# Attention denominators: DMA accumulation replaced by adds on GpSimd and more ones-matmuls

## The reference, cut to what matters

```python
att = jnp.einsum('bhgqd,bhkd->bhgqk', q, k) / scale
att = jax.nn.softmax(att, axis=-1)
y = jnp.einsum('bhgqk,bhkd->bhgqd', att, v)
```

## Time and profile before

| what | value |
|---|---|
| median of three runs | 3620.76 us |
| the profiled execution's own time | 3621.32 us |
| its span, first to last instruction | 3619.7 us |
| PE busy | 3493.0 us, 96% |
| VectorE busy | 2232.6 us, 62% |
| ScalarE busy | 1593.6 us, 44% |
| GpSimd busy | 1602.2 us, 44% |
| mean granted TensorE clock | 0.978 |
| adding DMAs (L706) | 128, 1024 KB each, median 7.2 us to landing |

### The profile page before, as it was taken

The page is one execution under the profiler, slowest core; times in us unless marked ns, Lnnn a source line. Parts: engine busy times, 40 slices in busy tenths (PEclk is TensorE's granted clock), DMA queues, the critical chain, the costliest instruction groups (busy, mean ns, idle before and its releaser), DMA issues. The chain is left out here.

```text
span 3619.7 us, 46130 instructions
## 1 busy us (share of the span) xinstructions
PE 3493.0 (96%) x17196; PEld 2320.7 (64%) x17196; DVE 2232.6 (62%) x3725; ACT 1593.6 (44%) x2990; POOL 1602.2 (44%) x700
## 2 busy tenths in 40 slices
PE   6999899999999999999999889799999999999999
PEld 4778455555555555555555268688888888887787
DVE  5541877777777777777777178544444444442627
ACT  3210266666666666666666533222222222213544
POOL 1111288898889989898899800000000000000010
PEclk8999699999999999999999989899999999999999
DMA  6662455656555555555554444711111111113222
GB/s 226 204 186 82 114 118 103 124 107 120 108 109 119 112 113 112 120 109 118 108 108 93 96 151 172 204 30 29 29 30 29 29 30 29 29 41 117 90 66 85
DMA packets 196074, 361.96 MB, mean 100 GB/s; under 512 B 41728, under 2 KB 122880, under 8 KB 175680
## 3 DMA queue, kind: packets, MB, share of 16 engines
q0 software_dynamic: 37104, 202.92, 24.7%
q1 hardware_dynamic: 156496, 154.69, 15.6%
q10 hardware_dynamic: 2304, 2.10, 0.2%
HBM read 162.13 MB, written 62.78 MB: 62 GB/s over the span
## 5 line engine op out<-in xcount | busy, mean ns | idle before, releaser
L772 DVE TENSOR_REDUCE att_chunk_max<-att_scores 128x1 f32<-128x512 f32 x2048 | 1268.9, 683 | 349.7 <-PE att_scores L843 347.5
L753 ACT ACTIVATE att_exp<-att_scores_T 128x512 f32<-128x512 f32 x2048 | 1042.7, 603 | 507.4 <-PE att_scores_T L857 503.4
L697 POOL TENSOR_TENSOR att_exp_pair<-att_exp 128x2048 f32<-128x2048 f32 x256 | 1198.6, 4727 | 133.1 <-ACT att_exp L753 132.8
L843 PE MATMUL att_scores<-att_k_stack,att_q_stack 96*128 96x512 f32 x2048 | 875.8, 450 | 16.7 <-DMA att_q_stack<-q_scratch 12.9
L857 PE MATMUL att_scores_T<-att_q_stack,att_k_stack 98*128 98x512 f32 x2048 | 745.3, 402 | 3.3 <-ACT att_exp L753 3.2
L843 PEld LDWEIGHTS att_scores<-att_k_stack,att_q_stack 96*128 96x128 f32 x2048 | 392.1, 192 | 427.2 <-DVE att_chunk_max L772 267.9
L868 PE MATMUL att_y_acc<-att_exp,att_v_head 128*32 128x512 f32 x4096 | 494.4, 600 | 0.0
L857 PEld LDWEIGHTS att_scores_T<-att_q_stack,att_k_stack 98*128 98x128 f32 x2048 | 386.4, 189 | 148.4 <-ACT att_exp L753 63.5
L1229 POOL DMA_DIRECT2D inter_scratch<-gu_inter x84 | 45.2, 538 | 884.6 <-DVE gu_inter L1172 884.6
L1283 ACT ACTIVATE gu_magnitude<-gu_value 128x512 f32<-128x512 f32 x88 | 55.7, 633 | 516.7 <-DVE gu_value L1314 516.7
L1313 DVE TENSOR_TENSOR gu_rounded<-gu_up_acc,gu_rounded 128x512 f32<-128x512 f32 x88 | 60.9, 692 | 323.7 <-PE gu_up_acc L1348 323.7
(11 more groups left out here) (191 smaller groups left out, 4925.1 us busy)
## 6 DMA issues: line engine op xcount, KB each, us to landing
att_exp_pair<-att_exp_pair POOLq DMA_DIRECT2D x128, 1024.0 KB, 7.2
att_q_stack<-q_scratch SPq DMA_DIRECT2D x96, 256.0 KB, 5.7
shared_raw<-in_wd_t POOLq DMA_DIRECT2D x34, 256.0 KB, 3.5
qkv_x_tile<-in_x SPq DMA_DIRECT2D x16, 512.0 KB, 4.8
q_scratch<-qkv_qk_out_hi POOLq DMA_DIRECT2D x32, 256.0 KB, 3.1
q_scratch<-qkv_qk_out_lo POOLq DMA_DIRECT2D x32, 256.0 KB, 4.3
qkv_wqkv_raw<-in_wmod POOLq DMA_DIRECT2D x8, 1024.0 KB, 7.4
qkv_wmod<-in_wmod POOLq DMA_DIRECT2D x8, 1024.0 KB, 8.2
```

The lines of the kernel that those rows point to most:

```text
L697: nc.gpsimd.tensor_tensor(ps[PAIR_SLOT[j]][:], pr[2 * j % NP][:], pr[(2 * j + 1) % NP][:], ALU.add).then_inc(pair_done, 1)
L753: nc.scalar.activation(pr[k % NP][:, h * NB:(h + 1) * NB], stp[bank(u, c, GH * k + h)][:], ACT.Exp, scale=INV_SQRT_DH).then_inc(exp_done, 1)
L772: nc.vector.reduce_max(cmax[c % 2][:, q:q + 1], turn_buffer(u, c, q)[:], AX.X).then_inc(sm_done, steps_done(u, q))
L843: nc.tensor.matmul(turn_buffer(u, c, q)[:], qs[c % 4][0:SR, h, qt * P:(qt + 1) * P], ks[c // QB % 2][0:SR, kc * NB:(kc + 1) * NB], start=T ...
```

## The change

The four adding DMAs and their semaphores go. POOL now makes two sums of four tiles, P0+P1 into buffer 0 behind P1, and P2+P3 into buffer 2 behind P3. The other four pair sums go to PE as they are, so PE has ND = 6 groups per unit. Three of them are issued in the unit's own loop, behind the bursts of k = 10, 12 and 14 (`DEN_AHEAD`), three in the next unit behind k = 0, 2 and 4 (`DEN_LATE`). The trip moves up: the copy on ACT to k = 4, the reciprocal on DVE to k = 8, `y_out` on POOL to behind P3 and ahead of the second sum. SP stores y ahead of the next unit's maxima.

```diff
--- before.py
+++ after.py
@@ -465,19 +465,16 @@
     NST = 3
     TQ = 6
     NP, NS = 8, 5
-    PAIRS = KT // 2
+    PAIRS, QUADS = KT // 2, 2
+    ND = QUADS + PAIRS - 2 * QUADS
     PAIR_SLOT = (0, 1, 2, 3, 4, 1, 3, 2)
-    DMA_SUM = ((0, 1), (2, 3), (0, 2), (3, 2))
-    SUM_PAIRS = (1, 3, 3, 7)
-    DMA_AFTER = {1: 0, 3: 1, 4: 2, 7: 3}
-    QUAD_AFTER = 5
-    DEN_SLOT = (0, 4, 3)
-    ND = len(DEN_SLOT)
-    DEN_AT = (0, 2, 6)
+    DEN_SLOT = (0, 2, 4, 1, 3, 2)
+    DEN_AHEAD = (10, 12, 14)
+    DEN_LATE = (0, 2, 4)
     RP = 8
-    DEN_COPY = 6
-    RECIP_AT = 9
-    Y_AFTER = 5
+    DEN_COPY = 4
+    RECIP_AT = 8
+    Y_AFTER = 3
     DW = GH * NB // P
     TSTEP = 14
     PER = NTURN // KT
@@ -516,8 +513,7 @@
         sm_ready, sm_done = sem("scores_ready"), sem("scores_consumed")
         mT_hi, m_stored = sem("max_T_hi"), sem("max_rows_stored")
         pv_done, pair_done, den_done = sem("pv_done"), sem("pair_done"), sem("den_done")
-        quad_done = sem("quad_sum_done")
-        dma_sum = [sem(f"dma_sum_done{i}") for i in range(len(DMA_SUM))]
+        quad_done = sem("quad_done")
         y_copied, y_done, y_stored = sem("y_copied"), sem("y_done"), sem("y_stored")
         const_done = sem("consts_done")
         den_copied, den_stored, den_loaded = sem("den_copied"), sem("den_stored"), sem("den_loaded")
@@ -661,10 +657,9 @@
                     load_v((c // QB + 1) % 2, g + 1)
                 if not is_first(u):
                     den_trip(u - 1, (c - 1) % BODY)
+                    store_y(u - 1, (c - 1) % BODY, g if c % QB else g - 1)
                 if not beyond(u, 1):
                     store_max(u + 1, c + 1)
-                if not is_first(u):
-                    store_y(u - 1, (c - 1) % BODY, g if c % QB else g - 1)
 
             units(sp, unit)
             sp.wait_ge(last_y, 1)
@@ -676,38 +671,14 @@
             def pair(u, j):
                 pool.wait_ge(exp_done, NST + 2 * GH * (j + 1) + u * NX)
 
-                if j == 0:
-                    pool.wait_ge(den_done, 1 + u * ND)
-                elif j == 1:
-                    if u:
-                        pool.wait_ge(quad_done, u)
-                elif j == 2:
-                    if u:
-                        pool.wait_ge(dma_sum[3], u * 16)
-                elif j == 3:
-                    pool.wait_ge(den_done, 3 + u * ND)
-                elif j == 4:
-                    pool.wait_ge(den_done, 2 + u * ND)
-                elif j == 5:
-                    pool.wait_ge(dma_sum[0], 16 + u * 16)
-                elif j == 6:
-                    pool.wait_ge(dma_sum[1], 16 + u * 16)
-                elif j == 7:
-                    pool.wait_ge(dma_sum[2], 16 + u * 16)
+                if j in (0, 1, 2):
+                    pool.wait_ge(den_done, (1, 4, 6)[j] + u * ND)
+                elif j == PAIRS - 1:
+                    pool.wait_ge(den_done, ND + 2 + u * ND)
+                elif j in (5, 6):
+                    pool.wait_ge(quad_done, j - 4 + u * QUADS)
                 nc.gpsimd.tensor_tensor(ps[PAIR_SLOT[j]][:], pr[2 * j % NP][:], pr[(2 * j + 1) % NP][:],
                                         ALU.add).then_inc(pair_done, 1)
-
-            def sum_by_dma(u, i):
-                into, other = DMA_SUM[i]
-                pool.wait_ge(pair_done, NP // 2 + SUM_PAIRS[i] + 1 + u * PAIRS)
-                if i == 2:
-                    pool.wait_ge(dma_sum[0], 16 + u * 16)
-                    pool.wait_ge(dma_sum[1], 16 + u * 16)
-                pool.dma_start(ps[into][:], ps[other][:], accum_op=ALU.add).then_inc(dma_sum[i], 16)
-
-            def quad_sum(u):
-                pool.wait_ge(pair_done, NP // 2 + 6 + u * PAIRS)
-                nc.gpsimd.tensor_tensor(ps[4][:], ps[4][:], ps[1][:], ALU.add).then_inc(quad_done, 1)
 
             def y_out(u, c):
 
@@ -719,12 +690,12 @@
             def unit(u, c, g):
                 for j in range(PAIRS):
                     pair(u, j)
-                    if j in DMA_AFTER:
-                        sum_by_dma(u, DMA_AFTER[j])
-                    if j == QUAD_AFTER:
-                        quad_sum(u)
                     if j == Y_AFTER and not is_first(u):
                         y_out(u - 1, c - 1)
+                    if j % 2 == 1 and j < 2 * QUADS:
+                        pool.wait_ge(pair_done, NP // 2 + j + 1 + u * PAIRS)
+                        first = ps[PAIR_SLOT[j - 1]]
+                        nc.gpsimd.tensor_tensor(first[:], first[:], ps[PAIR_SLOT[j]][:], ALU.add).then_inc(quad_done, 1)
 
             pool.sem_inc(pair_done, NP // 2)
             units(pool, unit)
@@ -871,13 +842,12 @@
 
             def denominators(u, i):
 
+                if i < QUADS:
+                    pe.wait_ge(quad_done, i + 1 + u * QUADS)
+                else:
+                    pe.wait_ge(pair_done, NP // 2 + QUADS + i + 1 + u * PAIRS)
                 if i == 0:
-                    pe.wait_ge(dma_sum[2], 16 + u * 16)
                     pe.wait_ge(den_copied, u + 1)
-                elif i == 1:
-                    pe.wait_ge(quad_done, u + 1)
-                else:
-                    pe.wait_ge(dma_sum[3], 16 + u * 16)
                 part = ps[DEN_SLOT[i]]
                 for h in range(GH):
                     ins = nc.tensor.matmul(dp[h * DH:(h + 1) * DH, :], ones[:], part[:, h * NB:(h + 1) * NB],
@@ -912,8 +882,10 @@
                                 by_v(u, c, g, k - b)
                             elif not is_first(u):
                                 by_v(u - 1, (c - 1) % BODY, g, KT - b)
-                        if k in DEN_AT and not is_first(u):
-                            denominators(u - 1, DEN_AT.index(k))
+                        if k in DEN_AHEAD:
+                            denominators(u, DEN_AHEAD.index(k))
+                        if k in DEN_LATE and not is_first(u):
+                            denominators(u - 1, len(DEN_AHEAD) + DEN_LATE.index(k))
                     ahead_turn()
                     scores_t(u, c, k, 3)
                     if transposing:
@@ -931,7 +903,7 @@
             units(pe, unit)
             for b in (2, 1):
                 by_v(NU - 1, (NU - 1) % BODY, HKV - 1, KT - b)
-            for i in range(ND):
+            for i in range(len(DEN_AHEAD), ND):
                 denominators(NU - 1, i)
 
 
```

## The result

| | median | range | runs |
|---|---|---|---|
| before | 3620.64 us | 3620.05 to 3621.32 | 4 |
| changed | 3687.26 us | 3686.13 to 3688.77 | 4 |

The ratio is 1.0184, 95% interval 1.0171 to 1.0198: slower by 1.8%, as forecast (3687). The profiled execution has a span of 3685.4 us against 3619.7, so +65.7 for a predicted +66.0.

A forecast was written before the change was run, and what follows sets the result against it. PE was taken to bound the attention, busy 1434.74 of 1438 us. Groups +80.0, reciprocal -2.8 and the end -11.2 sum to +66.0, giving 3687 us, 1.8% slower; own range 3676 to 3698, stated range 3668 to 3712.

The forecast's parts named there:

- A group costs 0.86 us and nothing covers it: PE, units 0 to 30: 93 more groups of ones-matmuls, each lengthening its step in full, +80.0 us.
- The reciprocal at k = 8 saves 0.09 per unit: VectorE: moving it from k = 9, among maxima PE waits for, saves 0.09 us in 31 units, -2.8 us.
- POOL's sums come in time: POOL: each sum is ready before PE's group needs it, the second with 2.7 us to spare; cost 0.
- The adding DMAs do not slow the engines: Attention: PE and POOL run no faster once the 1 MB adding DMAs are gone; 0 us.
- The end gives back 11.2: Last unit: PE's last group starts 11.2 us earlier without waiting for an adding DMA; bounds -14 and -8.5.
- The seam's clock counts nothing: After the attention, 2062 to 2098 us: granted clock 0.58 after idle PE; counted 0, some 7 us open either way.
- The trip's row loads take 3.7 without the DMAs: Four row loads bringing back the reciprocals before y: 3.7 us instead of 6.9 once no adding DMA runs beside them.
- rival A: Row loads still take 6.9 us, so PE stops 0.5 to 1.4 us at k = 12: +15 to +43, 3709 us; chance 0.14.

The follow-up runs named there:

- the version with four groups behind the last burst: Kernel before, last unit only: third and fourth adding DMAs and the sum of P4 and P5 left away, P4 to P7 sent to PE as groups; 3609.96 us.
- the version with one edit at the end: Kernel before, last unit only: fourth adding DMA left away, P6 and P7 sent to PE as two groups; 3613.88 us, ratio 0.9979.

## Why the prediction was right, point by point

The sum was right term by term, so the mechanism is right and not only the number. That it came within 0.3 us is in part luck: the trace is 0.3 above it until the last unit, 0.6 above it in the last unit, and 1.2 below it behind that.

- *A group costs 0.86 us and nothing covers it.* Shown: 0.86 to 0.88 by leaving out one, and three, per unit. The term was +80.0; leaving the three out took 80.2 away.
- *The reciprocal at k = 8 saves 0.09 per unit.* The step from 8 to 10 is 6.07 instead of 6.15 in the trace, and 6.16 with the reciprocal back at k = 9. The run with it back and y late is 1.9 us above the changed kernel, with ranges that overlap, so the size (2.8) is supported by the traces and not settled by the times.
- *POOL's sums come in time.* Right, with 3.0 us to spare for 2.7 predicted. The working has a slip: P1 ends at 17.6 and an add takes 4.6, so the first sum ends at 22.2 and not at 22.5 (22.3 in the trace). Nothing rests on it, since y waits for its rows behind it. That this is the tightest place is shown by four runs: a reciprocal one key tile later costs 29 us, a DMA that makes y 5.0 us late costs 77, and both cost about nothing once y stands behind the sum.
- *The adding DMAs do not slow the engines.* Shown.
- *The end gives back 11.2.* 10.6 in the trace. In it P7 ends 55.8 us behind the burst of k = 0 instead of 59.2, since POOL no longer waits there for a DMA (2.96 us in the kernel before); the other 7.2 are the adding DMA itself. Of the two, the part of the DMA is shown on the kernel before (6.75); the part of POOL's chain rests on the version with four groups behind the last burst, where 2.0 more came, less than 3.4, while PE's clock was lower. The figure of the Trainium skill for the DMA (page "DMA: Bandwidth & Descriptors", section "Anatomy of one DMA — SWDGE (gpsimd) path"), with -8.4, was further off.
- *The seam's clock counts nothing.* What lies behind the start of the last group got 1.2 us shorter, well inside the 7 us that were left open.
- *The trip's row loads take 3.7 without the DMAs.* Right (3.6), so rival A falls, but the reason had a gap: I took the loads for what suffers, and the store ahead of them suffers more when it is the one that falls into the traffic. Rival A's price of 15 to 43 us for a late y holds where it was tested: the reciprocal at k = 9 makes y 4.3 us late in the unit shown (3.2 in rival A) and costs 28.9. What I had no price for is the delay of the store, 77.

## What to carry to other kernels

Where one engine is busy without a gap, find a place where the same extra work is already done in some rounds and not in others: the distance between two repeated instructions with and without it is its price, and it held here within 3% (0.86 read off, 0.86 and 0.88 measured). Work moved from a hidden queue to such an engine costs its full time here, however much traffic it saves. Moving the last round alone to the other form takes the gain at the end without that price.

## What was not expected

- An 8 KB store issued 0.9 us behind a 1 MB adding DMA takes 6.3 us instead of 1.4. The DMA share of that run is only 0.22 on the mean of the attention, but 0.86 in the 6.3 us of this store, so the share has to be read over the stretch of the small transfer itself. This agrees with the Trainium skill, page "DMA: Bandwidth & Descriptors", section "Issuing engines are not separate DMA queues": transfers of all queues share the same engines.
- Two adding DMAs of 1 MB issued in a row take 7.0 us for the first and 11.4 for the second, where a single one takes 7.2. A plan that puts one more of them on the way to PE has to count that.
- In the profiled executions PE's clock falls in the last unit for one burst in the kernel before (3.6 us instead of 1.92), for two in the version with one edit at the end, and for three in that with four groups behind the last burst. What decides how often is not shown, and a forecast of the end is no surer than that.
